# A decoder layer in one program: cross-attention scores of two head pairs as one unit, on 32-row tiles of the array

## What is computed

```python
x = _layernorm(x + _L0_attn_ref(x, Wq, bq, Wk, bk, Wv, bv, Wo, bo))
x = _layernorm(x + _L0_xattn_ref(x, ctx_1024, ctx_1024, mask, w_q, w_k, w_v, w_o))
x = _layernorm(x + _L0_ffn_ref(x, w_gate, w_up, w_down))

# _L0_xattn_ref, 16 heads of D_K = 16; key and value have 64 rows
scores = jnp.einsum('bhqd,bhkd->bhqk', Q, K) / jnp.sqrt(jnp.float32(D_K))
scores = jnp.where(mask, jnp.float32(-1000000000.0), scores)
attn = jax.nn.softmax(scores, axis=-1)
out = jnp.einsum('bhqk,bhkd->bhqd', attn, V)
```

## Time and profile before

| | |
|---|---|
| median of 3 runs | 1032.99 us (1032.22 to 1035.34) |
| the profiled execution, its own time | 1029.18 us |
| its span, first to last instruction | 1027.4 us |
| TensorE (PE) busy | 977.1 us, 95% |
| VectorE (DVE) busy | 745.2 us, 73% |
| ScalarE (ACT) busy | 613.2 us, 60% |
| GpSimd (POOL) busy | 347.2 us, 34% |
| mean granted TensorE clock | 0.993 |

### The profile page before, as it was taken

How to read it: one execution, slowest core, us unless ns; L and a number is a source line. 1 busy time by engine, 2 the same in 40 slices (tenths; PEclk the granted TensorE clock), 3 DMA queues, 4 the chain that set the end, 5 groups by cost and what they waited for, 6 DMA issues and landing times.

```text
span 1027.4 us, 17715 instructions
## 1 busy us (share of the span) xinstructions
PE 977.1 (95%) x6128; PEld 506.1 (49%) x6162; DVE 745.2 (73%) x1634; ACT 613.2 (60%) x878; POOL 347.2 (34%) x440
## 2 busy tenths in 40 slices
PE   6788999999999999999999999999999999999986
PEld 3533455454654546445564445643645443535554
DVE  3798787768876788657987689774788558834487
ACT  2266775349663486545863458655495459763575
POOL 3225037513242355513135134540305213150202
PEclk9999999999999999999999999999999999999999
DMA  7519202111120211001210111010110100010001
GB/s 221 121 47 112 35 22 82 63 39 45 64 67 1 53 34 61 21 1 58 81 49 6 42 50 49 29 52 1 53 37 1 52 1 22 1 42 1 1 1 42
DMA packets 52565, 45.18 MB, mean 44 GB/s; under 512 B 12800, under 2 KB 51456, under 8 KB 52480
## 3 DMA queue, kind: packets, MB, share of 16 engines
q1 hardware_dynamic: 50624, 40.90, 13.9%
q0 software_dynamic: 1536, 3.15, 1.8%
q10 hardware_dynamic: 320, 0.00, 0.0%
HBM read 14.49 MB, written 4.19 MB: 18 GB/s over the span
## 4 chain that ended last, share of the span: by engine, by line
PE 83%; DVE 4%; ACT 4%; POOL 3%; DMA 2%; issue 2%; SPq 1%; ACTq 0%; POOLq 0%; DVEq 0%
PE ps L856 13%; PE ps L841 12%; PE ps L825 11%; PE ps L645 9%; PE ps L656 7%; PE ps L764 6%; PE ps L676 4%; PE ps L803 4%; PE ps L776 3%; PE ps L741 3%; PE ps L828 2%; POOL xt L626 2%; ACT probs L948 2%; PE ps L750 2%; PE ps L812 2%; DVE shift L1154 2%
## 5 line engine op out<-in xcount | busy, mean ns | idle before, releaser
L1154 DVE TENSOR_REDUCE shift<-ps 128x1 f32<-128x512 f32 (+5 forms) x688 | 382.8, 596 | 107.3 <-PE ps L828 69.5
L948 ACT ACTIVATE probs<-ps 128x1024 f32<-128x1024 f32 (+3 forms) x384 | 300.8, 810 | 206.5 <-PE ps L841 204.4
L609 POOL TENSOR_SCALAR_AFFINE_SELECT probs<-probs 128x512 f32<-128x512 f32 x128 | 81.7, 640 | 467.2 <-ACT probs L948 467.2
L825 PE MATMUL ps<-k_stack,q_stack 96*128 96x512 bf16 (+3 forms) x768 | 215.6, 330 | 3.7 <-DMA k_stack<-part_sb 3.3
L841 PE MATMUL ps<-q_stack,k_stack 97*128 97x512 bf16 (+3 forms) x768 | 182.4, 326 | 14.9 <-ACT probs L948 7.8
L856 PE MATMUL ps<-probs,v_aug 128*32 128x512 f32 (+3 forms) x1536 | 163.6, 499 | 1.5 <-POOL probs L609 1.4
L825 PEld LDWEIGHTS ps<-k_stack,q_stack 96*128 96x128 bf16 x768 | 72.7, 98 | 104.9 <-DVE shift L1154 30.2
L841 PEld LDWEIGHTS ps<-q_stack,k_stack 97*128 97x128 bf16 x768 | 61.0, 98 | 116.2 <-ACT probs L948 41.8
L828 PE MATMUL ps<-causal,ident_h 128*128 128x128 bf16 x512 | 105.4, 221 | 0.0
L626 POOL TENSOR_SCALAR xt<-xt,mv,rstd 128x256 f32<-128x256 f32 x84 | 101.8, 1224 | 2.2
L621 POOL TENSOR_TENSOR rstd<-veps,half_c 128x4 f32<-128x4 f32 (+1 forms) x27 | 26.0, 965 | 143.0 <-DVE veps L1113 142.9
(11 more groups left out here) (185 smaller groups left out, 1404.7 us busy)
## 6 DMA issues: line engine op xcount, KB each, us to landing
k_stack<-part_sb SPq DMA_DIRECT2D x192, 64.0 KB, 2.6
q_stack<-part_sb SPq DMA_DIRECT2D x144, 64.0 KB, 2.6
xt<-in_x SPq DMA_DIRECT2D x8, 512.0 KB, 4.6
out_x<-xt SPq DMA_DIRECT2D x7, 512.0 KB, 3.1
q_stack<-part_sb POOLq DMA_DIRECT2D x48, 64.0 KB, 6.6
part_sb<-in_x SPq DMA_DIRECT2D x6, 512.0 KB, 4.0
q_stack<-shiftT SPq DMA_DIRECT2D x128, 1.0 KB, 1.7
y<-in_x SPq DMA_DIRECT2D x2, 512.0 KB, 5.1
```

The lines of the kernel that those rows point to most:

```text
L609: pool.affine_select(out=blk, in_=blk, compare_op=ALU.is_ge, fill=0.0, base=0, pattern=[[0, HG], [1, P]], channel_multiplier=-1).then_inc( ...
L825: mm = pe.matmul(ps[:, u.bank, j * w:(j + 1) * w], q_stack[0:KR, c, h, qb % TH * P:(qb % TH + 1) * P], k_stack[0:KR, h, k0:k0 + w], start= ...
L948: act.activation(probs[:, n % 2, 2 * pair:2 * pair + 2, 0:BANK - off], ps[:, u.bank:u.bank + 2, 0:BANK - off], ACT.Exp).then_inc(probs_rea ...
L1154: dve.tensor_reduce(first[:, k0 // BANK, heads[0]:heads[-1] + 1, qb % TH], ps[:, u.bank, 0:len(heads) * w].rearrange("p (h w) -> p h w", w=w),
```

## The change

Three edits go together.

- A `score2` unit now covers two head pairs (`SCORE2_PAIR`), each in a bank of its own: the unit takes two neighbouring banks, as self-attention scores do. Where a part had 8 units of one pair, it has 4 of two pairs; a part of 256 queries has 4 units as before, whose two pairs now lie in two banks instead of in two halves of one.
- The float32 multiplication of a pair reads only the 32 partitions of its two heads, `rows = slice(i * D, (i + 2) * D)`, and no longer all 128. The two pairs of a unit stand on neighbouring 32-partition groups. The two bfloat16 multiplications of mask and shift come first, the two float32 ones after them. One exponential takes both banks.
- `ORDER` is another one throughout. The rule when `pv2` and `turn2` come within the chain is written for units of two pairs.

```diff
@@ -26,6 +26,7 @@
 SCORE_BANKS, SUM_BANK = [0, 2], 4
+SCORE2_PAIR = 2
@@ -36,45 +37,45 @@
 ORDER = (
-    "r7r6r7r6rr7r5r7rr6w7w5rr3r7gw5r6r2r5rr7r6r5m7m6m5m3w7m6gw2m5m7m1m3m6m5m7r2gm1m3w6r0m6w7m5a0m6a2m7m5m6rm7m3ao"
+    "r7r6r7r6rr7r5r7rgr6rr7r5w3gr2r6r1rr7m7m6w5m3m7m2m5m6m1m3m7w0r2m5r6m1m3m7w0m2w5m6w0m1w5m7a2r6w5a0gw7aa2m6wm5a"
...
@@ -177,6 +178,9 @@
+    def banks_of(u):
+        return 2 if u.kind in ("scores", "score2") else 1
+
@@ -187,9 +191,9 @@
-        for p in range(0, H // 2, m):
+        for p in range(0, H // 2, SCORE2_PAIR):
             units += [Unit("score2", b, (p, r), "act")]
-            if p // m in ((3, 5, 7), (2,))[m - 1]:
+            if p // 2 in ((1, 2, 3), (2,))[m - 1]:
                 units += [sums.pop(0)]
                 units += [turns.pop(0)] if len(turns) > len(sums) + 1 else []
@@ -260,12 +264,11 @@
-        if u.kind == "scores":
-            u.before = [owner[k] for k in (u.bank, u.bank + 1) if k in owner]
-            owner[u.bank] = owner[u.bank + 1] = u
+        if u.kind == "scores" or u.taker:
+            banks = range(u.bank, u.bank + banks_of(u))
+            u.before = [owner[k] for k in banks if k in owner]
+            owner.update((k, u) for k in banks)
         if u.taker:
-            u.before = [owner[u.bank]] if u.bank in owner else []
-            owner[u.bank] = u
@@ -756,19 +759,22 @@
                 elif kind == "score2":
                     p0, r = u.idx
-                    m = share(b, r)
+                    w = BANK // share(b, r)
                     pe.wait_ge(dve_taken, find["max2T", b, r].taken)
-                    for j in range(m):
-                        p, at = p0 + j, slice(j * BANK // m, (j + 1) * BANK // m)
-                        e, i = 2 * p // HC, 2 * p % HC
-                        pe.matmul(ps[:, k, at], k2[:, e, i:i + 2, :].rearrange("p h k -> p (h k)"), R.q2T[:, e, here(u)],
+                    at = [ps[:, k + j, 0:w] for j in range(SCORE2_PAIR)]
+                    for j in range(SCORE2_PAIR):
+                        p = p0 + j
+                        pe.matmul(at[j], off_pick[:, 2 * p:2 * p + 2, :].rearrange("p h k -> p (h k)"), maskT[:, columns(b, r, 0)],
                                   start=True, stop=False)
-                        mm = pe.matmul(ps[:, k, at], off_pick[:, 2 * p:2 * p + 2, :].rearrange("p h k -> p (h k)"),
-                                       maskT[:, columns(b, r, 0)], start=False, stop=True)
+                    for j in range(SCORE2_PAIR):
+                        e, i = 2 * (p0 + j) // HC, 2 * (p0 + j) % HC
+                        rows = slice(i * D, (i + 2) * D)
+                        mm = pe.matmul(at[j], k2[rows, e, i:i + 2, :].rearrange("p h k -> p (h k)"), R.q2T[rows, e, here(u)],
+                                       start=False, stop=True)
                 elif kind == "pv2":
                     g0, r = u.idx
                     m = share(b, r)
-                    pe.wait_ge(act_taken, find["score2", b, (2 * g0 + m, r)].taken)
+                    pe.wait_ge(act_taken, find["score2", b, (2 * (g0 + m - 1), r)].taken)
@@ -913,7 +919,10 @@
-                    ins = act.activation(*several(u, R.p2), ACT.Exp)
+                    at = p % R.p2.shape[1]
+                    w = BANK // share(b, r)
+                    ins = act.activation(R.p2[:, at:at + SCORE2_PAIR, here(u)],
+                                         ps[:, k:k + SCORE2_PAIR, 0:w], ACT.Exp)
```

More of the change, by code:

```diff
@@ new lines @@
+    "0m7m6m3r5m7oam6a0m5m7m3a0m6am5m2om7wm6m5a0rm3ga0r7om6aoom5a0m7m6m3m5a0m7am6a2m5a0m7m3m6m2m5m1wao7m0oa2a2w6om"
+    "7am5m3a0om6rm7a0m5r2m6agm3woa0m7m5a2m6a0oa2m7m5m6o1grm7oa2om6m5a0a2m7m6m5orga0m7w6m5m3w2m1m7oa2m6m5a0m7m6am5"
+    "w3a0m7m6w2m5m3a0m7oagm6m5a0a2oam7a0a2m6m5m1am7m3ooom6m5a0a2m7a0o6m5a2m7m1om6m5m7wa2a0oxm6a2m7m5a0oa2r6m7a0m5"
+    "r3am7m6w2oa0m7w6m5xm3w2a0m7m5am6om7a0m6m5a2om7aa0m6a2w5m7r1m6m7m5m3oam6m7wa0oa2m5aoa0m7a2ao6oa0a2m5m7aor6a0m"
+    "5a2m7om6aa0m5m7a2oom6m5aa0w7a2r6m7w5aw3ro6oa0w7m5a2em6aoa0m7a2m6am5m1om7om6om5m3a0o7r6p7p5m3a0m7m6bm5p3p7p6p"
@@ new lines @@
+    "5a0rga2pm7r6m5ooa0pra2m7m6r5a0m7m6m3op7m6m5m2p3m7m6m1m5p3p7p6a0m5a2p7m6p5p1p7a2p6p5p0aoom7a2p6a0m5m7m6p2p0m7"
+    "p6p2p7am6p5p0em7p6bm5p7p3m6m5p7a0a2p6oaga0m7a2m5p6ap1m7oom6m5a0p7a2m6m5m7p1op6m5p7o6rgpm5pa0m7a2om6a0r3m5a0o"
+    "m7m6ra0m5oa2m7a0pm6pr5a0m7m3rr2om7m6m5p3m2p7m6m1m5m3p7m6m2p0ap5gm3p1m6m7p2m0p3p5p6rm7p1r2p7m6ra0pr5m7a2aoa0p"
+    "p6r3a0m5om7am6a0a2gm5oap7a0m6a2m5oom7ar6pm5a0r7a2m6po1p0goaop7a2p5p6pm7a0aa2r5m6a0apr3oop2a0m7m5p6m3p2m7oa0a"
+    "p5m6a2r7p5a0ao6oa0pa2pm7m6p5p1om7m3m6p2p7m5p6m3am2a0p7m6gp5m7a0papgm6p3p5ooa0p7m5p3a0op6p7m5a0a2po7m6oa0a2m5"
@@ new lines @@
+    "oa0pr7m6m5ta2m7om6a0m7m5op7p6a0axm5a2m7p6m7m5m3p2m7p6r5m3a0p7p6ep5p3m7oaa0r6m5m3p7a0ap6p5m3m7ooa0p6m5m3a0m7m"
+    "6p0p2m7xp6p0m7p6p5m7m3p0m7m6p5p7p6am5p7a0p6oa2m7m5p6p1m7a2om6m5m0p1p7o6p5p3a0poa2m7ba0m6oa2r5m7a0pm6oa2m7m6m"
+    "5om7a0am6r5pa2r7rr6pm5m7a0oaa2m6p5m7m1p0a2m6rm7p5m6p3p7m6m2p1ap0m5cp6m3m2p7m5p3p1p2opa0r7a2pap6goa0m7m5op6ro"
+    "a2m7paa0r5a2pp7p6p1ap3o5poa0a2oaa0m7m6a2am5pp1p0rop7a2m6m5om7oa0m6p5aa2m7p6a0o5aoa0a2pm7m6om5aa0m3r2m7a0pp6p"
+    "5gm3p1m7m2m3om6m7ap5a0m3p2m6m5op7m6oa0o5p7rppp6a0a2p7op6p5p3p2m1r0p7m6p5m3p2p7m6opm5a0m7ra2r6a0a2om7gm5pm6a0"
@@ new lines @@
+    "a2m7om6aa0m7a2m5m6p1ap0ooa0a2m7am6p5m7a0ta2p6p7m5aoa0p7p6a2p5p7oop6a0p5p7a2o6m5m1m7p0oom6m7m5p0p2m7m6m5gp1m7"
+    "p2m7a0p6m7p5m3rp0m7a2p6p7p5m6p7a0p5m6a2om7p5p3m6m2a0m7m5m6p3ep7m6m5m2p3p7a0m6opaa2a0apm7m6m5m3m2oa0m7m6m5r1m"
+    "7a2oam6a2a0m5oapa0m7rm6a2or5apm7m1m6om5a2r7m1m6p0p5go7a2am1m0p6m5p7p3m2m1m0op6p7m5m3p2m6m1p5m7gp0p6p5a2r7a0p"
+    "om7m6pp5aa2p1r0obgm7a2am6m5a2a0am7oa2gpr6a0oxapm7p5p3p2m6p1o7r0poa2m6a0pap7p5p3p2p6m1r3pm7ooa0a2pp6am5p1m3m2"
+    "m0oop7m5r6p3a0m7o5m6p3m7p2m5a0p6m7ppr3p5m6m2a0tp7om5a0p7p6p3p2m7r6a0oa2pm7a0m6pm5om7a0a2m6m5m7a0am6m5om7m6a0"
@@ new lines @@
+    "m5m3oa0cm7am6p5p2m3ea0m7m5m6p2a0m7m6m5p3m7op6aa0m7p5oa0ap6p7a0p5a2p6m7oom5a0m6m7m3p2o5m6a0p7m3ooa0p7m6a2m5m7"
+    "p0p2m7m6m5p1p2m7a0m6p5m7m6m3p2p0m7p6m5p7p3a0p6m7m5p3oxa0m7m6r5m3p2a0m7p6m5m3m2oaom7a0m6m5p3m7m6p2a0p5m7p6aa0"
+    "a2poam7a0m6a2r5m1am0poa2om5m7m6oa2am1r0ra2m7m6pr5a0o7parom6m3r2m7a0m5p6p3oa0m7am6a2p5m1m7p3rm6m2m0p1p7m5p6m3"
+    "p2m1p7p5p6a2ap0ppor7p6op5oa0m7a2ppp6p5ap7grp1gr0rpa2r7a0o6pp5p3m2p1p7oap6pm5a0a2om7aa0m6a2oapp3p2gobm5m7a0p6"
+    "om5m7a2a0p6m5o7m3p2m5p1m7oa2m6a0p5pa2rpom7p6a0oa2p6p5a0p7a2m6p1p0aoa2m7m6a0p5am7m6p3p5m7cp6oa0a2poaa0m7a2m6m"
@@ new lines @@
+    "5atm1m0opor7om6a2grm5m1r0a2m7m6o5p1rp7oa0m7p6a0a2m7p5m7m6m1op7a2p6p5a0p7p6ea2p5m7p1op6a2m7m5m1op7m6a2m5p0p2m"
+    "7p6m5m7p0p6m7p5p0m7m6p5am7ga0p6p5a0m7p6m5p3aooa0m7p6m5p3m7a0m6am5p3a0p7p6p5m7a0paoa2m7a0oam6oa2m5pr1m7o0a2m6"
+    "am5r1om7a2m6gr5a0opaa0a2m7oam6pr5a0m7m3m6m5p2m7m1p0oa2m6p5m7p0m1m6m3gp7gm2m1p5m6p0p7ap5m3m2op1p7p6pa2a0pp7p6"
+    "o5aoa2pa0aom7a2a0pm6ap5m3op2p7a0om6p5opm7a2a0pp6o5m3om7a0p5p2p7p6a0a2ppp7m5om6m1p3op5bp6p7a0p5a2p7pa0pp6m5m7"
+    "p3om6m2a0p3p5p7p6apm5a0a2r7m6r1r3r2m5oaa0m7m6pm3m2m5a0aom7m6a0m3m2p1p5om7a0m6p5p3am7p6a0m7om5p6a2p7aoa0p6p5p"
@@ L78 @@
+    "5v7v3v5p6v7u2p3p5v7p6u0u2v0ppu2u7u0v2v0u7u6v5u7v0pu7v6v5u7pv6u5v7p6p5uv7v6up5vuvp7p6p3p2up1p5p7p6p0vu6vpu7pp"
+    "6p5u3pu2u7u6v1pp5p0p3p2u7ppp6p5p7v3up2p1v7v0v6v5ppp2uu3p7u5v1up6p5up3vvp7u6v5u2v1p3u7vpu5u6vv7v5v3v7v5pu6tuv"
+    "7vuvtt"
 )
```

43 lines of the change are left out of this document (5 added, 38 removed).

## The result

The changed kernel takes 1007.52 us (median of 4 runs, 1005.54 to 1008.86), the kernel before 1033.45 us in the same comparison; the ratio is 0.973 (95% interval 0.9704 to 0.9755). Timed again with 6 runs beside 17 of before it is 0.9716 (0.9691 to 0.9741). So the change saves 26 to 29 us where 16.5 were forecast. The forecast was put on a median of 1032.99 us for the kernel before; 0.973 of that is 1005.1 us, under the lower end of the range, 1007 us.

What follows compares the result with a forecast made beforehand. TensorE, busy 95%, was taken to set the end until 975 us, VectorE counting too after that. 1029.2 - 20.0 + 1 + 1.5 + 1 = 1012.7 us; -16.5 us put on the median gave 1016.5 us, range 1007 to 1028.

Steps and rivals of the forecast that it cites:

- 27.6 - 10.8 = 16.8: Score units on TensorE: 27.6 us saved by side-by-side float32 multiplications, less 10.8 us for tiling changes and late weights.
- Both rivals on overlap: Float32 row tiles on TensorE: only halves overlap, 1030 us, chance 0.05; or no overlap at all, 1044 us, chance 0.06.
- what the order moves: New ORDER: 3.2 us less on TensorE from 15 fewer runs of L856, +1 us at the start, +1.5 at the end.
- new waits: Score units waiting for bank pairs shared with self-attention: +1 us, with 0 and +10 as ends.
- -3.2 us of tiling changes: Groups of L856 on TensorE: 15 runs fewer, each 0.21 us of tiling changes and weights.
- +1 at the start: Ahead of the first L825: about 2.6 us of work no longer fills the DMA wait; ends 0 and +2.6.
- +1.5 at the end: Around the first `up`: about 11 us comes ahead, 8 or a little more goes from behind; ends -3 and +6.
- 12 us of gaps: TensorE between 100 and 950 us: only 12 us idle in 850, held against the rival that waits eat the gain.
- better than forecast: Rival for the whole kernel: below 1008 us, by hidden tiling changes or an order that also closes gaps; chance 0.08.
- 48 to 50 us: Sign at the start: the first scores, which wait for the DMA of the shift, stand still at 48 to 50 us.

## Why the prediction was right or wrong

**The units: right, to the tenth.** A unit of 512 columns takes 1.58 to 1.60 us where 1.60 was forecast, seven of the eight units of 256 take 0.95 to 0.96 us in the second profile where 0.96 was; the row tiles run side by side; they save 17.1 us (the kernel on 128 partitions against the changed one), forecast as 27.6 - 10.8 = 16.8. Both rivals on overlap are refuted, by the timeline and by the kernel on the same 32 partitions. The rule of the page "TensorE: Matmul & The Clock Gate" of the Trainium skill (Part 3), multiplications strictly in order, would have meant three passes, 1.3 us, if each float32 one issued both its passes; the trace has 1.06. The rule of the page "TensorEngine Tiling (Array Packing)" of the Trainium skill (Key Properties), a drain at each change of tiling, agrees with the 0.10 us that padding `max2` gave back per change. The single exponential costs and brings nothing measurable.

**The order: wrong, and this is the step that failed.** The step was "what the order moves" with "new waits": -3.2 us of tiling changes, +1 at the start, +1.5 at the end, +1 of waits, about nothing in sum. Measured, with the old units in the new table, it is -12 us. The miss is in the middle stretch, where the step gives -2.2 us (-3.2 and +1) and the runs have -11.6. These 11.6 us are of three kinds.

- *Changes of tiling and weights, 3.9 us.* In the traces the new table has 15 runs of L856 fewer in the middle (176 to 161) and 35 changes of tiling fewer in all (497 to 462): 35 x 0.10 and 15 x 0.03. That is the forecast term, 3.2 us, and a little more.
- *Work that left the middle, 2.9 us.* 16 rows of TensorE now lie outside it, ten of them five `max2` units (54 of 64 in the middle before, 49 now) that stand in the end stretch. No term of the forecast had that.
- *Waits, the remaining 4.8 us.* Only 1.7 of them are idle time on the page (7.4 to 5.7 us). Most of the rest are short waits, which the modelled end of the instruction ahead covers. Read from start to start, less the streaming time and the usual price of a change, all waits over 0.03 us add up to about 21 us before and 16.5 us with the new table, an estimate from the starts of the rows. The forecast gave the waits ends of 0 and +10 us and no end below zero.

The forecast read 12 us of gaps in the earlier trace rows as proof that there was little to lose. Some 3 of them were idle time only because rows are missing, and the short waits do not stand in them at all. The rival "better than forecast" named closed gaps, with no price. Which of the table's many moves closes the waits was not tested.

**New waits: none in the new table, many without it.** The share of a shared bank pair was priced at +1 us by the rate of self-attention. In the new table there is no such cost (over the span L847 waits for L957 5.0 us in 14 waits, has 7.8 in 15). In the old table the same units lose all of their 17 us, to idle time on TensorE (15.3 us in the middle against 7.4) and to the half-clock stretches that followed it. The shared bank pairs show in both: where the first letter was kept, self-attention's units waited 5.1 us for the exponential of a score unit (L924); where the second was kept, score units waited 2.5 us for VectorE to take row maxima away (L1163). How much of the loss they are was not measured by itself. The two parts of the change are not a sum: the table gives 12 us to the old units, the units give 15 us with the new table (1022.8 to 1007.9) and nothing or less with the old.

**Start and end.** Up to the 17th group the profiles of before take 113.5, 113.7 and 117.9 us, those of the changed kernel 116.3 and 120.4: some 3 us more, forecast +1, but single executions differ by 4. In the first 60 us the half-clock stretches add up to 10.2 us in all three of before and to 13.7 us in both of the changed kernel. The first scores start at 51.9 and 54.1 us (before: 48.7, 49.3, 52.5), so the sign "48 to 50 us" failed. The end takes 103.8, 105.6 and 103.8 us before. With the old units in the new table it takes 105.9 us (one profile), 1.5 us more than their mean, forecast +1.5; with the new units 106.7 us (10.2 of them at half clock) and 102.0 us. So the new order does cost something at the end, and the units' own saving there hides it. That the size is the forecast one may be luck: single executions differ by 2 us, and the five `max2` units that moved there were in no term.

**The scale.** The forecast was summed against one profiled execution (1029.18 us) and shifted to the median. Three profiled executions of before average 1031.2 us and two of the changed kernel 1008.6: 22.6 us, which is 26.0 in the middle less 3.3 at the start. The timed executions, which show no inside, differ by 26 to 27 us. These 4 us stay open, and as much is left for the old units in the new table: -11.6 in the middle, +2.5 at the start and +1.5 at the end are -7.6 us, and the medians differ by 12.0. A spread of landing times and of half-clock stretches like the ones seen would be enough, but no run shows it.
